# Sparse feed-forward with linear attention on one Trainium2 core: six small moves between VectorE, ScalarE, GpSimd and TensorE

## The reference

```
xn   = layernorm(x)
q, k, v = xn @ Wq, xn @ Wk, xn @ Wv        # 16 heads of 32, rotary on q and k
per head and chunk:
  out = (q * q_decay) @ kv + ((q @ k.T) * dmask) @ v
  kv  = r_C * kv + (k * k_decay).T @ v
attn = rms_norm(out, rms_w) @ Wo
z    = xn @ ternary(W_syn).T + b_syn       # 2048 wide
hidden = where(z >= 204th largest of its row, relu(z), 0)
ffn  = layernorm(xn + hidden @ ternary(W_out).T + b_out) * gamma + beta
result = x + attn + ffn
```

## Time and profile before

| what | value |
|---|---|
| median of 3 runs | 1027.73 us (1027.38 to 1028.2) |
| the profiled execution | 1028.2 us, span 1026.1 us |
| PE busy | 950.6 us, 93% |
| DVE busy | 844.6 us, 82% |
| POOL busy | 741.6 us, 72% |
| ACT busy | 588.5 us, 57% |
| mean granted TensorE clock | 0.97 |

### The profile page before, as it was taken

How to read it: one execution, slowest core, us unless ns; L and a number is a source line. 1 busy time by engine, 2 the same in 40 slices (tenths; PEclk the granted TensorE clock), 3 DMA queues, 4 the chain that set the end, 5 groups by cost and what they waited for, 6 DMA issues and landing times.

```text
span 1026.1 us, 19222 instructions
## 1 busy us (share of the span) xinstructions
PE 950.6 (93%) x6771; PEld 480.0 (47%) x6771; DVE 844.6 (82%) x2289; ACT 588.5 (57%) x780; POOL 741.6 (72%) x650
## 2 busy tenths in 40 slices
PE   1767699999999999999999999999999999999874
PEld 0333345545555555545555555554555555554431
DVE  3587778888888888889888888889888888888873
ACT  4876666555556656555556656655555665655421
POOL 1325667777888777787898777778788877777532
PEclk9987899999999999999999999999999999999987
DMA  9784664754644664564544555555544565555322
GB/s 313 253 200 65 127 125 95 115 108 99 99 92 90 113 113 90 108 114 97 110 85 93 103 113 93 104 114 109 98 101 91 88 114 108 94 108 104 76 49 61
DMA packets 328786, 113.69 MB, mean 111 GB/s; under 512 B 314736, under 2 KB 314992, under 8 KB 327792
## 3 DMA queue, kind: packets, MB, share of 16 engines
q1 hardware_dynamic: 326576, 108.25, 53.8%
q10 hardware_dynamic: 2112, 4.19, 1.2%
HBM read 25.38 MB, written 8.39 MB: 33 GB/s over the span
## 4 chain that ended last, share of the span: by engine, by line
PE 84%; DVE 1%; issue 1%; ACT 1%; DMA 0%; POOL 0%; POOLq 0%; DVEq 0%; ACTq 0%
PE proj L766 42%; PE p_ffn L867 22%; PE p_wo L909 8%; PE p_av L837 3%; PE sbank L828 3%; PE p_av L892 3%; PE sbank L774 1%; PE sbank L930 1%; DVE area L1232 0%; DMA area<-hl 0%; PE sbank L942 0%; ACT hl L498 0%; PE p_wo L848 0%; DVE Pr L1149 0%; ACT pair_a L366 0%
## 5 line engine op out<-in xcount | busy, mean ns | idle before, releaser
L766 PE MATMUL proj<-wqkv,xT 128*128 128x512 f16 x1152 | 259.7, 383 | 0.7 <-DVE wqkv L1035 0.4
L766 PE MATMUL proj<-wsynT,xT 128*128 128x512 f16 x1024 | 247.3, 385 | 1.3 <-DMA wsynT<-xr 0.9
L867 PE MATMUL p_ffn<-woutT,area 128*128 128x512 f16 x1024 | 235.4, 384 | 8.3 <-DMA area<-hl 8.3
L766 PEld LDWEIGHTS proj<-wqkv,xT 128*128 128x128 f16 x1152 | 112.0, 99 | 128.7 <-issue 4.6
L867 PEld LDWEIGHTS p_ffn<-woutT,area 128*128 128x128 f16 x1024 | 98.8, 101 | 118.8 <-DMA area<-hl 8.5
L766 PEld LDWEIGHTS proj<-wsynT,xT 128*128 128x128 f16 x1024 | 93.4, 99 | 116.7 <-issue 19.4
L483 ACT ACTIVATE diag<-ident,c 128x128 bf16<-128x128 f32 x32 | 12.8, 402 | 204.8 <-DVE c L1165 204.8
L657 POOL TENSOR_TENSOR hl<-area,hl 128x2048 f16<-128x2048 f32 x30 | 122.4, 4081 | 4.4 <-ACT hl L498 4.3
L1090 DVE SCALAR_TENSOR_TENSOR area<-proj,c,gb 128x512 f32<-128x512 f32 x128 | 95.3, 744 | 31.6 <-PE proj L766 28.8
L570 POOL TENSOR_TENSOR c<-c 128x1 f32<-128x1 f32 x32 | 17.5, 548 | 135.8 <-DVE c L1080 135.8
L1184 DVE MAX8 cand<-area 128x8 f32<-128x128 f32 x512 | 110.4, 278 | 0.0
(11 more groups left out here) (195 smaller groups left out, 1625.2 us busy)
## 6 DMA issues: line engine op xcount, KB each, us to landing
xr<-in_L_attn_x_dram SPq DMA_DIRECT2D x32, 256.0 KB, 3.0
out_dram<-pair_b SPq DMA_DIRECT2D x32, 256.0 KB, 2.0
area<-in_L_ffn_W_out_dram SPq DMA_DIRECT2D x3, 1024.0 KB, 6.1
woutT<-in_L_ffn_W_syn_dram ACTq DMA_DIRECT2D x2, 1024.0 KB, 11.7
area<-in_L_ffn_W_syn_dram ACTq DMA_DIRECT2D x2, 1024.0 KB, 16.7
woutT<-in_L_ffn_W_out_dram SPq DMA_DIRECT2D x2, 1024.0 KB, 6.4
area<-in_L_attn_Wq_dram SPq DMA_DIRECT2D x1, 1024.0 KB, 6.8
area<-in_L_attn_Wk_dram SPq DMA_DIRECT2D x1, 1024.0 KB, 9.3
```

Source lines behind the costliest of these rows:

```text
L766: last = nc.tensor.matmul(bank, xT[:, b.par, k, :], w, start=m == 0, stop=m == len(pairs) - 1)
L867: last = nc.tensor.matmul(p_ffn, hT[:, k, :], woutT[:, k % NB, :], start=k == 0, stop=k == 2 * NB - 1)
```

## The change

- `diag` is made by VectorE, between the two splitting operations and `att_factor` in `factors`, no longer by ScalarE.
- GpSimd multiplies by gamma before it adds up the squares, no longer after.
- `failures` stands after matmul 14 of the network, no longer after 16.
- `factors_spread` stands after the first projection for tile 2 as well.
- VectorE copies the failure count before the last z chunk, no longer after.
- The two last operations of `fail` take their second operand as a tensor, no longer as a scalar.

```diff
@@ scalar step @@
-                if u:
-                    wait(act, "factor_step", u, 3, 1)
-                    wait(act, "factors_spread", u, 1, 0)
-                    nc.scalar.activation(diag, ident, ACT.Copy, scale=step_up).then_inc(S["diag_ready"], 1)
@@ gpsimd step @@
                 if b:
                     rotary(b)
+                if d:
+
+                    wait(pool, "yn_ready", d, 1, 1)
+                    nc.gpsimd.tensor_tensor(y, y, gam, ALU.mult).then_inc(S["yg_ready"], 1)
                 if t:
...
                     nc.gpsimd.tensor_tensor(sq[:, 0, :], sq[:, 0, :], sq[:, 1, :], ALU.add).then_inc(S["sq_sum"], 1)
-                if d:
-
-                    wait(pool, "yn_ready", d, 1, 1)
-                    nc.gpsimd.tensor_tensor(y, y, gam, ALU.mult).then_inc(S["yg_ready"], 1)
@@ tensor network, step @@
-                        if k == NB and between:
+                        if k == NB - 2 and between:
                             between()
...
-                        if n == (2 if b.n == 2 else 0):
+                        if n == 0:
                             factors_spread()
@@ vector step @@
                     wait(dve, "rstdR_ready", u, 1, 1)
-                    wait(dve, "diag_ready", u, 1, 0)
...
+                    wait(dve, "factor_step", u, 3, 1)
+                    nc.vector.tensor_scalar(diag, ident, step_up, None, ALU.mult).then_inc(S["diag_ready"], 1)
                     wait(dve, "factor_step", u, 3, 2)
                     nc.vector.tensor_scalar(att_factor, mant, wo_back, None, ALU.mult).then_inc(S["factor_step"], 1)
...
-                if t and t.n > 1:
-                    z_chunk(t, 3)
                 if u:
                     wait(dve, "fail_all", u, 1, 1)
                     nc.vector.tensor_copy(failint[0:1, 0:1], p_wo[0:1, 0:1]).then_inc(S["fail_count"], 1)
+                if t and t.n > 1:
+                    z_chunk(t, 3)
...
-                    nc.vector.tensor_scalar(s1, m8, val, None, ALU.is_gt).then_inc(S["top_step"], 1)
+                    nc.vector.tensor_tensor(s1, m8, val, ALU.is_gt).then_inc(S["top_step"], 1)
                     wait(dve, "top_step", t, 12, 12)
-                    nc.vector.tensor_scalar(fail, pre, s1, None, ALU.max).then_inc(S["fail_ready"], 1)
+                    nc.vector.tensor_tensor(fail, pre, s1, ALU.max).then_inc(S["fail_ready"], 1)
```

## The result

| what | before | after |
|---|---|---|
| median | 1027.97 us (1027.38 to 1030.28, 4 runs) | 1056.41 us (1055.22 to 1057.39, 4 runs) |
| ratio to before, 95% interval | | 1.0272 (1.0251 to 1.0293) |
| profiled execution, span | 1028.2, 1026.1 us | 1057.11, 1055.3 us |
| mean granted TensorE clock | 0.97 | 0.971 |

What follows compares the result with a forecast made beforehand. In full steps only TensorE's own work counts; other engines set the pace at start and end. Span 1026.1 + 11.5 + 3.7 - 0.3 = 1041.0, run 1043.1, on the median's scale 1042.6 us, range 1034 to 1049.

Steps and rivals of the forecast that it cites:

- Gamma, 0.41 a step, 11.5 us: GpSimd's last addition of squares comes too late for TensorE's `ss` in 28 steps, 0.41 us each (7.3 to 14 in all).
- The two changed operations should take off 0.05 each ... So I take no stall: At `failures`, tensor forms shorten `fail`, so its near meeting with TensorE costs nothing; bounds 0 and 0.1 a step.
- `failures` becomes a wait too: Rival: `fail` misses its slot by up to 0.1, a second stall partly replacing that at `ss`; 1045 at most, no chance given.
- The loop: VectorE's copy waits for `failures` behind the stall, so VectorE, ScalarE and GpSimd start equally later; the stall isn't given back.
- Start, 3.7 (2.5 to 4.6): At tile 2 TensorE waits about 2.6 us before the k projection, then runs partly at half speed; 3.7 us lost.
- `diag` is held: `diag` on VectorE stands still while GpSimd's L638 runs, by the shared-port rule; 0.41 a step, without it about 0.27.
- Masking 0.1 later: VectorE's masking in each full step starts at about 510.2 instead of 510.09, moving GpSimd's queue by between -0.05 and +0.2.
- slack of 0.92: In a full step, GpSimd's last addition of squares ends at 531.33 and may end at 532.25 without delaying the network.
- The register load: Its 0.62 wait on VectorE before L1221 runs behind the z chunk, and up to 0.4 of it goes.
- The end, -0.3: In the last tiles earlier `failures` gains 0.43 and `diag` ahead of masking costs 0.15 to 0.2 each; bounds -0.6 and +0.3.
- The range: 1034 to 1049: low end 6.5 for the steps and no start, high end 14 + 4.6 + 0.3 and half a us.

Runs made afterwards that it cites:

- after_scalar: The changed kernel with the last two operations of `fail` back in scalar form; 1045.61 us, ratio 1.0181.
- before_gamma_first: The kernel before with only gamma's product moved ahead of the two additions of squares; 1038.06 us, ratio 1.0102.
- after_gamma_last: The changed kernel with gamma's product back behind the two additions of squares; 1060.73 us, ratio 1.0314.
- three_left: The changed kernel with scalar `fail`, gamma behind the squares and tile 2's `factors_spread` behind the projections again; 1030.05 us, ratio 1.0031.
- before_k14: The kernel before with only `failures` two matmuls earlier; 1027.58 us, ratio 1.0002.

## Why the prediction came out too low

- **Gamma, 0.41 a step, 11.5 us: right.** With the small edits beside it, as the term has it, the step is 0.43 longer than before (`after_scalar`). Gamma's own part was forecast at 0.31 and is 0.37 alone (11.0 us) and 0.33 beside the small edits (10.3 us, 1045.61 - 1035.34). That the stall isn't given back is shown: in `before_gamma_first` none of the 27 steps is shorter than 28.98.
- **"The two changed operations should take off 0.05 each ... So I take no stall": this step failed.** One of them takes 0.76 more, the pair 0.71, and the stall that I took for nothing came in every full step. I had the row that tells of it, L1225 held by L638, and the rule, and I used both for `diag` and masking alone; for `fail` I looked at the width, one column, and at the time of the constant forms. The question that I left out is what GpSimd does at 506.6 in the trace of before. Its rows hold the answer, with an operation of two SBUF inputs (L1339) that took 0.56 beside it and 0.25 at the end, where GpSimd has nothing to do:

```profile
505.21 2.27 POOL L604 TENSOR_TENSOR area<-area 128x512 f16<-128x512 f32 x2
...
505.86 0.56 DVE L1339 SCALAR_TENSOR_TENSOR sel<-iota,c,top 128x32 f32<-128x32 f32 x1
...
990.61 0.25 DVE L1339 SCALAR_TENSOR_TENSOR sel<-iota,c,top 128x32 f32<-128x32 f32 x1
```

  The price in the changed kernel is 10.8 us, the larger part of the missing 13.8; the start is most of what is left.
- **The rival "`failures` becomes a wait too" was mis-sized.** It had the place, but bounded the delay of `fail` at 0.1 and had each us of it taken off the wait of `ss`. The runs bear out that it is taken off in part: step 29.11 without the hold and 29.47 with it, 0.36 for a delay of 0.71.
- **The loop was seen in part.** I had GpSimd's queue run on from VectorE's copy, but I closed it through masking and ScalarE only. `after_gamma_last` shows what follows from the whole circle: with `fail` held, gamma ahead of the squares saves 4.3 us where alone it costs 11.
- **Start, 3.7 (2.5 to 4.6): too low.** The pause was 3.19 where I had 2.6: TensorE was through with the q projection at 97.39, not 98.4, while the matmul behind `diag` went at 100.58, sooner than my 100.9. So the pause isn't what was short in the sum. The clock was: the granted 0.50 lasted over all of the k projection, not over eight of twelve matmuls, and that gave 4.99 late at L494, 5.3 and 5.9 us in the two pairs of runs. The mechanism is as forecast.
- **`diag` is held: right** in 18 of the 28 full steps (0.87, ending with L634, the L638 of before); in the other ten it took 0.33 behind an L1222 that was held in its place. Masking 0.1 later is right too: in `three_left` it starts 6.68 behind `ss` (median of the steps), before the change 6.57. What I had not is its way to `fail`: I measured the delay against GpSimd's slack of 0.92, and not against L1339 and the meeting of `fail` and `failures`.
- **The register load.** I let up to 0.4 of it vanish behind the z chunk. It does in 18 of the 28 steps. In the other ten it takes 0.88 to 1.05 us (0.30 to 1.05 over all; 0.31 to 1.00 before), L1222 comes just behind L634 and stands still, and the step is 29.68 instead of 29.37. One such step:

```profile
290.30 0.15 DVE L1218 TENSOR_SCALAR c<-c 128x1 f32<-128x1 f32 x1 [0.36 <-DVEq L1216]
...
290.54 1.05 POOL L634 TENSOR_TENSOR pair_c<-v,kdec 128x512 f32<-128x512 f32 x1
290.55 1.05 DVE L1222 SCALAR_TENSOR_TENSOR c<-c 128x1 f32<-128x1 f32 x1
...
291.70 0.33 DVE L1165 TENSOR_SCALAR diag<-ident,c 128x128 bf16<-128x128 f32 x1
```

L1165 behind it takes 0.33, since L634 is done. Nine of the 27 steps are of this kind; at 0.31 more they are 2.8 us of the whole.
- **The end, -0.3:** +0.2 in the one pair of traces, within what the clock does there.
- **The range.** My high end, 14 + 4.6 + 0.3 + 0.5, gives 1047.1; the 1049 of the text is more than its own sum.

The parts don't add up, as the circle wants: gamma 11.0, tensor form 17.2, the start 5.3 and the three small edits 3.0 would be 36.5; together they cost 28.4 by the first comparison, 29.3 against 1027.1.

No version here beats the kernel before; `before_k14` equals it.

## What to carry to other kernels

Before a VectorE operation gets a second operand from SBUF, look up in the trace which GpSimd operation runs at its time: in these traces its price was what was left of that one, though it had one column itself. When two engines wait for each other once in a step, find the whole circle first; a delay on it is paid in each step, a second one beside it only in part, and a move that shortens the circle can gain although it lengthens a wait. An operation that waits shouldn't be moved ahead of one that doesn't.

## What was not expected of the hardware

- A one-column VectorE operation with two SBUF operands stood for 0.97 us beside a 128x512 operation of GpSimd, and took 0.16 behind it. The guess on one column took 1.06 where it started with GpSimd's product and 0.16 where it had ended before it.
- A 128x128 `tensor_scalar` to bf16 was held in the same way (0.87 beside L634, 0.33 behind it, 0.29 with GpSimd idle), though it has one tensor operand.
- Loading one number into a register took 0.30 to 1.05 us from step to step, and about as much in the kernel before (0.30 to 1.00); in the changed kernel it went with steps of two lengths.
- After a pause of 3.19 us TensorE worked at a granted clock of 0.50 for the whole k projection; 15 matmuls took 6 us.
